# Raw rows turned ahead of the norm, one choice over 16 tiles, sums in column groups, gates and lambda moved into the expert loop

## What is computed

```python
def _L0_ffn_ref(x, Wr, br, W1, b1, g1, be1, W2, b2, g2, be2):
    logits = xt @ Wr + br                      # xt: 2048 rows of layernorm(x)
    p = softmax(logits); probs, idx = top_k(p, 2)
    probs = probs / probs.sum(-1)
    h = layernorm(relu(xt @ W1[e] + b1[e])) * g1[e] + be1[e]     # 8 experts, 512 wide
    y = layernorm(relu(h @ W2[e] + b2[e])) * g2[e] + be2[e]
    out = sum over the two chosen e of gate_e * y_e
x = x + 0.5 * ffn(layernorm(x)); x = x + attn(layernorm(x)); x = x + 0.5 * ffn(layernorm(x))
```

## Time and profile before

| | |
|---|---|
| median of the runs | 447.54 us (446.53 to 448.34) |
| span of the profiled execution | 444.6 us |
| outside the span | 2.9 us against the median |
| TensorE busy, matmuls | 395.1 us, 89% of the span |
| VectorE busy | 348.4 us, 78% |
| ScalarE busy | 286.7 us, 64% |
| GpSimd busy | 246.8 us, 56% |
| mean granted TensorE clock | 0.965 |

### The profile page before, as it was taken

The page is one execution under the profiler, slowest core; times in us unless marked ns, Lnnn a source line. Parts: engine busy times, 40 slices in busy tenths (PEclk is TensorE's granted clock), DMA queues, the critical chain, the costliest instruction groups (busy, mean ns, idle before and its releaser), DMA issues.

```text
span 444.6 us, 11683 instructions
## 1 busy us (share of the span) xinstructions
PE 395.1 (89%) x3605; PEld 278.5 (63%) x3606; DVE 348.4 (78%) x1302; ACT 286.7 (64%) x589; POOL 246.8 (56%) x348
## 2 busy tenths in 40 slices
PE   7989999999898857889888889976899899999984
PEld 7735487877676744556564656554577677878733
DVE  5886578887959886878897988976688968788865
ACT  1395687755676754787677777764765467667630
POOL 8685554436461136374847566576634758555540
PEclk9996999999999955999999999999999899999999
DMA  7920114554443411000000001001121221111127
GB/s 219 335 96 14 35 49 143 181 178 158 121 144 112 170 37 35 21 8 20 25 13 25 24 21 33 25 27 36 56 60 34 72 64 56 53 59 47 37 72 244
DMA packets 25862, 35.17 MB, mean 79 GB/s; under 512 B 4282, under 2 KB 18546, under 8 KB 24659
## 3 DMA queue, kind: packets, MB, share of 16 engines
q1 hardware_dynamic: 20866, 24.62, 16.7%
q0 software_dynamic: 4944, 9.90, 7.6%
HBM read 15.45 MB, written 18.24 MB: 76 GB/s over the span
## 4 chain that ended last, share of the span: by engine, by line
PE 51%; DVE 20%; issue 9%; POOL 8%; ACT 5%; DMA 3%; DVEq 1%; SPq 1%; POOLq 0%; ACTq 0%
PE bank L972 11%; PE bank L991 10%; PE bank L981 5%; DVE mx L2134 4%; POOL xr_scratch L459 3%; PE bank L1181 3%; PE bank L2495 2%; PE bank L1900 2%; DMA early<-y_scratch 2%; PE bank L1176 2%; ACT early L1712 1%; PE bank L1918 1%; POOL orr L1658 1%; PE bank L1852 1%; DMA y_scratch<-yo,dest_u 1%
## 5 line engine op out<-in xcount | busy, mean ns | idle before, releaser
L991 PEld LDWEIGHTS bank<-w2c,hT 128*128 128x128 f32 x624 | 76.5, 194 | 23.5 <-issue 22.6
L991 PE MATMUL bank<-w2c,hT 128*128 x624 | 78.1, 279 | 4.9 <-ACT hT L760 4.9
L972 PE MATMUL bank<-w1s,xT 128*128 x156 | 74.1, 596 | 0.7 <-DVE w2c L2369 0.6
L2134 DVE TENSOR_REDUCE mx<-bank 128x4 f32<-128x1024 f32 (+1 forms) x48 | 58.5, 1220 | 13.7 <-PE bank L1861 13.3
L1712 ACT ACTIVATE early<-bank 128x768 f32<-128x768 f32 x64 | 51.8, 812 | 23.7 <-PE bank L1908 23.0
L1377 DVE BATCH_NORM_STATS2 st<-wide 128x6 f32<-128x512 f32 x78 | 50.1, 683 | 19.8 <-ACT wide L754 19.7
L760 ACT COPY hT<-bank 128x1024 f32<-128x1024 f32 (+1 forms) x40 | 39.5, 988 | 34.0 <-PE bank L981 34.0
L513 POOL DMA_INDIRECT xgw<-xn_scratch,slot_u x39 | 37.4, 960 | 35.4 <-PE bank L961 24.3
L483 POOL DMA_INDIRECT y_scratch<-yo,dest_u x39 | 39.0, 1001 | 31.3 <-PE bank L981 16.8
L579 POOL DMA_INDIRECT yk<-y_scratch,posi x32 | 32.2, 1005 | 42.2 <-DMA y_scratch<-yo 17.4
L754 ACT ACTIVATE wide<-bank 128x1024 f32<-128x1024 f32 (+1 forms) x40 | 40.0, 1001 | 10.3 <-PE bank L972 9.6
(11 more groups left out here) (380 smaller groups left out, 893.4 us busy)
## 6 DMA issues: line engine op xcount, KB each, us to landing
xr_scratch<-row_buf SPq DMA_DIRECT2D x8, 1032.0 KB
xgw<-xr_scratch SPq DMA_DIRECT2D x39, 64.5 KB, 1.8
y_scratch<-yo SPq DMA_DIRECT2D x19, 128.0 KB, 1.8
w1s<-in_L_ffn_W_dram SPq DMA_DIRECT2D x1, 2048.0 KB, 9.9
early<-y_scratch SPq DMA_DIRECT2D x8, 256.0 KB, 3.4
xn_scratch<-row_buf SPq DMA_DIRECT2D x1, 1024.0 KB
out_dram<-xs SPq DMA_DIRECT2D x8, 128.0 KB, 2.6
row_buf<-row_buf SPq DMA_DIRECT2D x6, 128.0 KB
```

The costliest lines, as they stand in the source:

```text
L972: last = pe.matmul(bank[h_at[u] + j][:], xT[:, u, j, :], w1s[:, bass.ds(e * FF, FF)], start=True, stop=True)
L991: last = pe.matmul(o[:, j * DIM:(j + 1) * DIM], hT[:, u, j, c * P:(c + 1) * P], w2c[:, bass.ds(e * (FC * DIM) + c * DIM, DIM)], start=(c = ...
L2134: dve.tensor_reduce(mx[:, c:c + 2 * per].rearrange("p (a q) -> p q a", q=2), quad[:, low:low + 2, :].rearrange("p q (a e) -> p q a e", a=p ...
```

## The change

It rewrites the front of `f1` in these parts.

- The router weights are centred (`wrc`), the raw rows are turned as soon as the input is there, and the logits are scaled by the deviations afterwards. TensorE's opening warm matmuls are 15 instead of 30.
- The choice is one pass over 16 tiles. Rows are normed later: four tiles on VectorE behind the choice, twelve on ScalarE.
- W1's work stands ahead of the one-hots' matmuls. The W2 sums have four chunks in four column groups of the array, both halves ahead of the one-hots; the masks and products are rebuilt for that, and the products stand before the first gathered rows are turned.
- Loads of small parameters are regrouped; `g2b` is loaded later, lambda's inputs on SP's queue.
- The two exponentials are powers of e on GpSimd: the gates' between the gathers of pairs 2 and 3, lambda's ahead of the gathers of pair 4. Gates and lambda's sums move to VectorE's program behind the second body.

The diff, cut to its core:

```diff
-        N_IDENT, N_REP, N_EPS, N_MASK, N_CENTER, N_ROWS, NCONST, N_ORDER = 1, 2, 3, 5, 6, 12, 16, 17
+        OWN_MADE = 3
+        N_IDENT, N_EPS, N_CENTER, N_REP, N_ROWS, NCONST, N_ORDER = 1, 2, 3, 4, 10, 14, 15
...
@@ -521,13 +526,19 @@
                 pool.wait_ge(S["xTp"], p - 1)
                 for j in tiles[p]:
                     gather(2 * p + j, 2 * (p % 2) + j)
+                if p == 2:
+                    pool.wait_ge(S["top"], 1)
+                    pool.tensor_tensor(gden[:], euler[:], mw[:], ALU.pow).then_inc(S["gexp"], 1)
             F = sems["f2"]
-            pool.wait_ge(s_colc, 2 + NE)
+            pool.wait_ge(s_colc, 3 + NE)
             pool.memset(row_buf[1][:], 0.0).then_inc(F["base"], 1)
             pool.wait_ge(F["base"], 1)
             pool.memset(row_buf[1][:].rearrange("p (c w) -> p c w", w=ROW)[:, :, DIM], NOWHERE).then_inc(F["base"], 1)
             pool.iota(spare, pattern=[[P, 40]], base=YBASE + TOPK * TOK, channel_multiplier=1,
                       allow_small_or_imprecise_dtypes=True).then_inc(F["base"], 1)
+            pool.wait_ge(A["lam"], 1)
+            pool.tensor_tensor(lam_e[:], euler[:, 0:2], lam_s[:], ALU.pow).then_inc(A["lame"], 1)
+
             def gather_pair(p):
                 pool.wait_ge(S["xTp"], p + 3)
...
                         act.copy(be2p[:], bank[7][:, 0:DIM]).then_inc(s_colc, 1)
-                turned_rows(act, S, 3, first)
-                hidden_weights_back(act, range(0, 3))
+                act.wait_ge(s_rstd, 1)
+                for t in range(NORM_BY_VECTOR, TT):
+                    act.activation(xn[:, t, :], xs[:, t, :], ACT.Identity, scale=rstd[:, t:t + 1], bias=shift[:, t:t + 1]).then_inc(S["xn"], 1)
+                hidden_weights_back(act, range(NE))
...
-                scaled(0)
-                hidden_weights_back(act, range(3, 6))
-                scaled(1)
-                act.wait_ge(S["top"], 1)
-                act.activation(gden[:], mw[:], ACT.Exp).then_inc(S["gexp"], 1)
-                act.wait_ge(A["lam"], 1)
-                act.activation(lam_e[:], lam_s[:], ACT.Exp).then_inc(A["lame"], 1)
-                act.activation(spad, eps_c[:], ACT.Sqrt)
...
+                scaled(0, 0, 4)
                 own_rows(act, 0)
-                hidden_weights_back(act, range(6, 8))
+                own_rows(act, 1)
+                scaled(0, 4, 16)
+                scaled(1, 0, 16)
```

GpSimd's gathers, then ScalarE's front, above; TensorE's front and VectorE's choice:

```diff
                 pe.wait_ge(s_const, N_ROWS)
-                keep_warm(5, 5)
-                for g in range(1, 4):
-                    turn_rows(pe, S, g, first)
-                    logits(pe, S, g - 1, first)
-                    if g < 3:
-                        keep_warm(3, 5)
-                logits(pe, S, 3, first)
-                hidden_weights(pe, range(0, 3))
+                pe.wait_ge(s_colc, 1)
+                for g in range(4):
+                    logits(pe, S, g, first)
+                    keep_warm(3, 5)
+                keep_warm(6, 5)
+                hidden_weights(pe, range(0, 1))
...
-                hidden_weights(pe, range(3, 6))
-                weight_sums(pe, 0, range(FC))
+                hidden_weights(pe, range(1, NE))
+                weight_sums(pe, 0)
+                weight_sums(pe, 1)
                 for c in range(TOPK * TT):
...
-                hidden_weights(pe, range(6, 8))
-                pe.wait_ge(s_colc, 2 + 6)
-                weight_sums(pe, 1, range(FC))
 
...
 
+        NORM_BY_VECTOR = 4
+
         def first_routing(dve, S, step):
-            row_stats(dve, S, 0, 4)
...
+            dve.wait_ge(S["sd"], 4)
+            step(dve.reciprocal(rstd[:], sdev[:]))
+            all_rows = [P, TT, NE]
+            dve.wait_ge(S["lgp"], 4)
+            step.begin(dve.tensor_tensor(lg[:], raw_logits().rearrange("p (a b) -> p a b", b=NE),
+                                         rstd[:, :, None].to_broadcast(all_rows), ALU.mult))
+            dve.scalar_tensor_tensor(shift[:], mv[:, :, 0], -1.0, rstd[:], ALU.mult, ALU.mult).then_inc(s_rstd, 1)
...
-            choose(1)
...
+            for t in range(NORM_BY_VECTOR):
+                dve.tensor_scalar(xn[:, t, :], xs[:, t, :], mv[:, t, 0:1], rstd[:, t:t + 1],
+                                  ALU.subtract, ALU.mult).then_inc(S["xn"], 1)
 
             dve.wait_ge(S["rankp"], 1)
             dve.wait_ge(s_const, N_ORDER)
```

Gates and lambda on VectorE, the W2 sums, GpSimd's set-up and the warm matmuls:

```diff
             dve.tensor_scalar(slot_u[:], slot_i[:], TOPK * TOK - 1, 1, ALU.bitwise_and, ALU.logical_shift_right).then_inc(S["slot"], 1)
+            step(dve.tensor_scalar(eidf[:], eidf[:], float(2 * NE - 1), None, ALU.min))
+            step(dve.tensor_scalar(past8, eidf[:], float(NE), float(NE), ALU.is_ge, ALU.mult))
+            step(dve.tensor_tensor(eidf[:], eidf[:], past8, ALU.subtract))
             pack_experts(dve, S, step, 0, 40)
+
+        def own_gates(dve, S, step):
+            gates(dve, S, step)
+            dve.wait_ge(s_ld_a, 128)
+            step(dve.tensor_tensor(lam_p[:], lam_in[:, 0:4:2, :], lam_in[:, 1:4:2, :], ALU.mult))
+            dve.tensor_reduce(lam_s[:], lam_p[:], X, ALU.add).then_inc(A["lam"], 1)
+
+        def own_lambda(dve, step):
+            dve.wait_ge(A["lame"], 1)
+            step(dve.tensor_tensor(neg_lam[:], lam_e[:, 1:2], lam_e[:, 0:1], ALU.subtract))
+            step(dve.tensor_scalar(neg_lam[:], neg_lam[:], -LAMBDA_INIT, None, ALU.add))
 
         def vector_pair(dve, S, steps):
             ls = steps(dve, S["lstep"])
@@ -1482,6 +1496,7 @@
                 e = experts(dve, eid, 0, 2)
                 body(0, 0)
                 body(1, 1, e)
+                own_gates(dve, S, step)
             loop_end = BESIDE if first else PAIRS - 4
...
-            for c in chunks:
...
+                last = pe.matmul(bank[6 + h][32 * c:32 * c + 32, :].rearrange("p (a d) -> p a d", d=DIM), cols[:, c:c + 125:4],
+                                 w2s[:, 4 * h:4 * h + 4, c, :], start=True, stop=True, tile_position=(0, 32 * c))
+            last.then_inc(s_wmix, 1)
...
             pool.wait_ge(sems["f1"]["xn"], TT)
-            for j, w in enumerate((lq1, lk1, lq2, lk2)):
-                pool.dma_start(lam_in[:, j, :], w.rearrange("(o a) -> o a", o=1).to_broadcast([P, HD])).then_inc(s_lam, 16)
             order = weigh16.rearrange("p (a b) (c d) -> p a b c d", a=2, c=2)
...
             pe.wait_ge(s_const, N_IDENT)
-            for _ in range(30):
+            for _ in range(15):
```

More of the change, by code:

```diff
@@ L890, in moe_scalar @@
                     body(i * 2 + u, u)
+            if first:
+                gates_turned()
             left = [min(2, max(0, SLOT_TILES - 2 * p)) for p in range(PAIRS + 2)]
@@ L1493, in expert_loop_vector @@
                     e = experts(dve, eid, 2 * n - 2, PACK)
+                    if first and n == loop_end:
+                        own_lambda(dve, step)
                 body(n, n % 2, e[2 * at:2 * at + 2], k=left[n], kh=left[n + 1], beside=first)
```

215 lines of the change are left out of this document (102 added, 113 removed).

## The result

The kernel after takes 454.36 us (median of four runs, 453.97 to 457.06) beside 447.24 us of the kernel before (four runs, 446.53 to 448.34). The ratio is 1.0154, 95% interval 1.0105 to 1.0204: 7.1 us slower. The profiled execution spans 451.9 us, 7.3 more than the 444.6 of before. A second series gave 454.45 beside 448.73, ratio 1.012 (1.0095 to 1.0145).

What follows compares the result with a forecast made beforehand. The chain of waits bounds the kernel, priced by when pair 4's transpose starts: 3.7 us later, held by GpSimd's wait for lambda, plus 2.0 of lower clock, 5.7 on 447.5: 453.2 us. Range 449.5 to 457.3.

Steps and rivals of the forecast that it cites:

- The choice: VectorE's choice of experts: starts at 15.2 instead of 17.22, `picked` done at 19.9 against 23.8, 3.9 us earlier.
- The wait for normed rows: GpSimd builds the ordering weights only after all rows are normed, at 21.0; VectorE starts the ranks at 22.8, not 21.2.
- TensorE up to the slots: Last W1 expert ready at 29.4, W2 sums 1.8 us, slots from 31.2 to 36.4, slot numbers at 37.3.
- The first gather: GpSimd's set-up of 16.3 us bounds it: issued at 39.5 (G), before 40.22; ends 38.2 and 43.3.
- From there to the stall: Second-layer product at G+11.2, lambda's power at G+22.35, pair 4's second gather landed at G+26.5; TensorE stands 7.2 us.
- The clock: TensorE behind the stall at the lower clock: 2.0 us lost, at least 1.7 and up to 3.4.
- The slack: Each gather later than pair 4's has about 5 us of slack and adds nothing.
- serial sums: TensorE's W2 sums don't overlap and take 7.1 us: slots at 42.4, first gather 43.3, time 457.0 us; chance 6%.
- the early end of both terms: First gather at 38.2 (1.3 us less) and no clock loss (2.0 less): 449.9, with the range starting from 449.5.
- the freely started gathers: On GpSimd, gathers start while the lambda step waits: pair 4 transposed at 58.8, 3.5 us earlier, time 444.0; chance 12%.
- The lower clock in further places: TensorE slow also behind the slot matmuls or at the start: 2 to 3.5 us more, 456 us; chance 13%.
- later stages absorb the loss: Behind 110 us, VectorE and GpSimd end some waits, so part of the loss goes: 450.5 us; chance 7%.

Runs made afterwards that it cites:

- the filled stall: The kernel after, with 26 warm matmuls added on TensorE behind the second body, where it stood idle: 455.79 us, ratio 1.0151 to the kernel before.

## Why the prediction was right, and where its sizes were off

It said 453.2 us, slower, by a GpSimd wait for lambda that holds the gathers of pair 4. The measured time is 454.36, and the removal of that wait takes away the whole loss. Point by point:

- **The choice** ended 0.65 us later than put (20.54 for 19.9). The logits began at 10.47, not 9.9, and VectorE at 15.94, not 15.2. Its steps took 4.6 us for 4.4; the prediction's own terms, 15.2 and 4.4, add up to 19.6, so the 19.9 held 0.3 us that no term of it named.
- **The wait for normed rows** is there as told: GpSimd starts the weights at 21.72 (21.0), VectorE starts the ranks at 23.50 (22.8) after 1.84 us of idle. Only the start was late.
- **TensorE up to the slots**: W1's copy on ScalarE ready at 30.1 (29.4), sums 1.9 us (1.8), slots from 32.0 (31.2). The serial end of 7.1 us is excluded. By the factor 3.07 that the Trainium skill's "TensorE: Matmul & The Clock Gate" (Part 3, Measured speedup vs the span model) states for four row tiles, the prediction had made an estimated 2.3 us of the 7.1; here two halves went from 7.1 to 1.9, a factor of 3.7, so the trace doesn't bear that part out for column groups.
- **The first gather** is the term that was mis-sized: 40.71 for 39.5, later even than before. Half of it is the late start, the other the set-up, which took 17.1 us (23.35 to 40.42) for 16.3. So the front's gain of 3.2 us in the choice (23.76 to 20.54) arrived at the gathers as a loss of 0.5, and the first second-layer product won 2.6 us, not 4.3. The prediction took the 16.3 us from one trace as fixed; two steps of one form in it (L1835 and L1836, 128x1) take 0.22 and 1.26 us.
- **From there to the stall** the distances held: second product at G + 11.5 (11.2), the power's end at G + 22.5 (22.35), the second gather landed at G + 26.8 (26.5). The second transpose of pair 4 came at 67.52, 5.2 us late instead of 3.7: 1.2 by the gather, 0.3 by the chain. The hidden product behind it is 5.6 us late, because it follows a single transpose by 0.4 us; the prediction had no term for that.
- **The clock** took 2.0 us (7.5 at pair 5 less 5.6 at the hidden product), put at 2.0, and 1.9 to 2.2 by the filled stall.
- **The slack** of the gathers behind pair 4, put at about 5 us each, is 2.5 for pair 5. In the kernel after this cost nothing, since the stall at pair 4 gave all of them time.
- **Not in the sum** was that gates between two bodies cost VectorE's schedule 0.7 us even without the wait (a period of 5.4 for 4.7). In the kernel after this lies inside the stall.
- **Small slips of the sum**: with serial sums the slots are at 42.6 (37.3 and 5.3), not 42.4, and the early end of both terms gives 449.9, not 449.5. Neither moves the forecast.

Of the rivals, the freely started gathers didn't come: GpSimd took nothing past its wait. The serial sums didn't either. The lower clock in further places came and went with the profile: at the first hidden product in one of two, 1.4 us at the mark, within the scatter of the time. Nor did later stages absorb the loss: it is 7.7 us at the attention mark and 7.3 in the span.

## What to carry to other kernels

A wait in an engine's own program is paid by everything queued behind it, so before moving a small step to an engine that issues transfers, ask which transfer is next behind it and when the awaited value will exist; put such a step where that engine waits anyway. An earlier result is worth only what the next engine in line can take: here 3 us on VectorE ended behind a set-up on GpSimd which nobody had shortened. And look for the second wait (all rows normed) that an unrelated constant inherits when the work in front of it is reordered.

## What the runs showed of the hardware

GpSimd's clearings hold some VectorE steps until they end. In the kernel after, VectorE and GpSimd behind the ordering weights:

```profile
23.50 0.17 DVE L1326 TENSOR_SCALAR yk<-bank 128x16 int32<-128x16 f32 x1 [1.84 <-POOL yk L2474]
23.71 0.62 DVE L1327 TENSOR_SCALAR yk<-yk 128x16 int32<-128x16 int32 x1
24.36 0.97 DVE L1328 CAST yk<-yk 128x16 f32<-128x16 int32 x1
```

```profile
23.35 0.94 POOL L2475 MEMSET q<- 128x1024 f32 x1
24.35 0.95 POOL L2476 MEMSET k<- 128x1024 f32 x1
```

The first step reads the bank and takes 0.17 us in the middle of a clearing. The next two have both operands in SBUF, and end within 0.05 us of the end of the clearing beside them (24.33 and 24.29, 25.33 and 25.30); without a clearing beside them, in the kernel without the norm wait, each takes 0.17. That is 1.2 us on VectorE's way to the slots; it costs the kernel after nothing, because GpSimd's set-up bounds the first gather there. The 2.51 us step above is the same thing. The Trainium skill, "SBUF — State Buffer" (Who interferes with whom), says that a cast or a tensor_scalar can enter a mode in which it and a GpSimd step exclude each other for the whole instruction; the trace agrees for the clearings. It doesn't for the power, during which the 128x256 step took 0.29 us. And the step at 54.39 started 0.5 us ahead of the row of the clearing that held it, during that power: why it was held then and not with a gather behind the power stays open. The estimate that the prediction had worked out from this page, a set-up 0.5 to 1 us quicker, went the wrong way; it was 0.8 us slower.

The trace tells more of how VectorE stretches GpSimd's set-up. In both kernels three GpSimd steps, which all read SBUF, are stretched to over 1 us. Each starts during one of VectorE's three longest comparisons, two of 128x2048 and one of 1x768, which have both inputs in SBUF, and ends 0.1 to 0.4 us behind it:

```profile
29.18 1.26 POOL L1836 TENSOR_SCALAR mrow<-mrow 128x1 f32<-128x1 f32 x1
```

```profile
29.14 1.22 DVE L1348 TENSOR_TENSOR wide<-lo_f,iota_rep 128x2048 bf16<-128x2048 bf16 x1
```

In the kernel after the three take 1.26, 1.29 and 1.16 us, in the kernel before 1.06, 1.21 and 1.06. For these three the trace agrees with the rule that the prediction took from the Trainium skill's "SBUF — State Buffer" (SBUF: two separate sides), which the page limits to a GpSimd step that reads SBUF and starts second. So a set-up that starts elsewhere doesn't get clear of these comparisons; another of its steps is held by them.
